# Leaving out GpSimd's spacer memset behind the row gathers of thirteen of sixteen sequences

## The reference, cut to what matters

```python
# third layer: two of eight experts for each token, weighted, plus the shared experts p
y_sel = y_all[topk_idx, jnp.arange(T)[:, None], :]
y = (y_sel * topk_w[..., None]).sum(1).reshape(b, s, h)
y = y + p
...
# fourth layer: the gates come from the mean over a whole sequence of y
pooled = x.mean(axis=1)
logits = pooled @ gate_w.T + gate_b
...
gates = jax.nn.softmax(masked, axis=-1)
expert_out = jax.nn.gelu(jnp.einsum('bsd,eod->beso', x, expert_w) + expert_b[None, :, None, :], approximate=False)
return jnp.einsum('be,beso->bso', gates, expert_out)
```

## Time and profile before

| | |
|---|---|
| median of 3 runs | 590.78 us (590.07 to 592.22) |
| profiled execution, first to last instruction (span) | 585.8 us |
| what lies around the span | 590.78 - 585.8 = 5.0 us |
| POOL busy over the span | 232.9 us (40%), 319 instructions |
| PE busy over the span | 558.2 us (95%) |
| the 64 gathers of the last stage | starts from 468.9 to 566.6 us |

### The profile page before, as it was taken

One profiled execution on the slowest core, in us unless ns is written; L12 is line 12 of the kernel. 1 busy time (PEld: TensorE's weight loads), 2 busy tenths in 40 slices (PEclk: granted clock), 3 DMA queues, 4 the chain that ended last, 5 costly groups with the idle time before them and its releaser, 6 DMA issues.

```text
span 585.8 us, 11495 instructions
## 1 busy us (share of the span) xinstructions
PE 558.2 (95%) x3816; PEld 462.9 (79%) x3816; DVE 319.7 (55%) x967; ACT 242.6 (41%) x670; POOL 232.9 (40%) x319
## 2 busy tenths in 40 slices
PE   7999999988999999999999999999999999999895
PEld 4788887744999999988788978888888887776674
DVE  3877757676332225743537754444444444666564
ACT  1555444660211111115544245555555455443342
POOL 2312211042111121007545375555555078777860
PEclk9999999999999999999999999999999999999999
DMA  5960000185995522513396035555555324555562
GB/s 144 390 289 4 1 1 2 63 368 243 333 328 199 184 85 73 155 64 74 72 296 210 0 82 158 157 159 161 161 161 148 99 81 126 170 173 184 158 190 75
DMA packets 51158, 88.16 MB, mean 150 GB/s; under 512 B 9202, under 2 KB 41843, under 8 KB 49556
## 3 DMA queue, kind: packets, MB, share of 16 engines
q1 hardware_dynamic: 42980, 65.16, 31.6%
q0 software_dynamic: 8112, 22.16, 15.7%
HBM read 62.25 MB, written 25.04 MB: 149 GB/s over the span
## 4 chain that ended last, share of the span: by engine, by line
PE 74%; POOL 8%; DVE 7%; issue 4%; DMA 4%; ACT 2%; SPq 1%; POOLq 0%; ACTq 0%; DVEq 0%
PE psum L1326 10%; PE psum L1339 9%; PE psum L1498 9%; PE psum L1586 9%; POOL arena L924 6%; PE psum L1600 5%; PE psum L1182 5%; PE psum L1154 5%; PE psum L1515 4%; PE psum L1578 3%; DMA arena<-x,row_tok 2%; PE psum L1162 2%; PE psum L1661 1%; PE psum L1533 1%; POOL iota_i L954 1%
## 5 line engine op out<-in xcount | busy, mean ns | idle before, releaser
L924 POOL DMA_INDIRECT arena<-x,row_tok x71 | 68.3, 963 | 53.4 <-PE psum L1578 43.4
L924 POOL DMA_INDIRECT arena<-y_sorted,pos_k_i x64 | 64.4, 1006 | 34.7 <-issue 16.2
L1586 PE MATMUL psum<-big_w,arena 128*128 x284 | 73.0, 379 | 0.0
L1916 ACT ACTIVATE arena<-psum,arena 128x128 f32<-128x128 f32 x64 | 18.3, 368 | 106.4 <-PE psum L1326 84.7
L1661 PE MATMUL psum<-big_w,arena 128*128 x248 | 61.3, 379 | 0.0
L1326 PEld LDWEIGHTS psum<-arena,big_w 128*128 128x128 f32 x512 | 59.5, 192 | 1.7 <-issue 1.0
L1326 PE MATMUL psum<-arena,big_w 128*128 128x128 f32 x512 | 59.8, 275 | 0.8 <-DVE arena L2613 0.8
L1498 PE MATMUL psum<-arena,big_w 128*128 128x256 f32 x256 | 59.8, 381 | 0.2 <-ACT arena L1935 0.2
L1586 PEld LDWEIGHTS psum<-big_w,arena 128*128 128x128 f32 x284 | 53.7, 190 | 7.3
L1339 PE MATMUL psum<-arena 128*128 128x256 f32 (+1 forms) x256 | 57.7, 379 | 0.0
L2849 DVE SCALAR_TENSOR_TENSOR arena<-arena 128x128 f32<-128x128 f32 x71 | 20.8, 293 | 60.4 <-ACT arena L2002 57.2
(11 more groups left out here) (338 smaller groups left out, 996.3 us busy)
## 6 DMA issues: line engine op xcount, KB each, us to landing
y_sorted<-arena SPq DMA_DIRECT2D x71, 128.0 KB
big_w<-w SPq DMA_DIRECT2D x8, 1024.0 KB, 5.2
tokens<-x SPq DMA_DIRECT2D x4, 1024.0 KB, 13.2
x<-tokens SPq DMA_DIRECT2D x16, 256.0 KB, 2.6
z_kept<-arena SPq DMA_DIRECT2D x16, 256.0 KB
out<-arena SPq DMA_DIRECT2D x15, 256.0 KB
y_late<-arena SPq DMA_DIRECT2D x16, 128.0 KB, 1.7
big_w<-expert_w_t SPq DMA_DIRECT2D x1, 2048.0 KB, 8.0
```

The source lines that it names most:

```text
L924: pool.indirect_dma_start(dst, None, rows, bass.IndirectOffsetOnAxis(ap=idx, axis=0)).then_inc(done, 16)
L1586: mm = pe.matmul(bank[2 + i % RT][:, 0:2 * M1], c_gt[i % RT][:, k, :], mgu_s[:, k, bass.ds(e, 1), :].rearrange("p a m -> p (a m)"), start= ...
```

## The change

The call of space() in the last stage gets a condition. The memset, and POOL's wait for it, stay behind the twelve gathers of sequences 0 to 2, and go behind the 52 gathers of sequences 3 to 15. Gathers, their waits for d_z, and all other engines' programs are as before.

```diff
                 for n, k, done in parts:
                     gather_rows(yk[b % RT][:, 2 * n + k, :], y2_dram, pos_k_i[:, b * NB + n, k:k + 1], done)
-                    space()
+                    if b < RT:
+                        space()
```

## The result

The first runs of the changed kernel took 603.74 us in the median (601.26 to 606.12, 4 runs), those of the kernel before beside them 590.42 us (589.92 to 592.22, 4 runs): a ratio of 1.0215, 95% interval 1.0179 to 1.0250. That is slower, and outside the range that was given. So this part has two things to explain: what the change does, and what the first runs had that the later ones had not.

A forecast was written before the change was run, and what follows sets the result against it. POOL's spaced gathers were taken to bound the last stage from sequence 10 on, costing 3.67 us over the loop's beat. Removing that whole cost: 590.78 - 3.67 = 587.1 us, 0.6% less; range 586.0 to 591.0 us.

The forecast's parts named there:

- The bound in the kernel before: Last stage: POOL's gathers need 6.43 us per sequence, the loop 5.35, so POOL sets the beat from sequence 10 on.
- the lead: How far a sequence's last gather starts ahead of its sum: 10.42 us at sequence 3, 3.95 at sequence 9.
- The unspaced gap of 0.30 us: POOL's pause between gathers without a memset, taken from an earlier stage; the change saves 0.19 us per gather.
- 3.67 us: Last stage: what gathers cost over eleven steps, 62.52 us against 58.85; the most that faster gathers can give.
- The 5.0 us "around the span": Median of the runs above the profiled span of 585.8 us; claimed that nothing of it changes.
- What else feels it: Side effects: gather landing covered (4.84 us against a 7.2 us lead), DVE's sums not slowed by memsets, nothing gained in the loop.
- the beat of 5.35 us: Last stage: time per sequence of the loop without POOL, transposes to sum, expected to hold up to sequence 14.
- the eleven steps: PE's transposes from sequence 3 to 14, last stage: 62.52 us before, 58.85 at the loop's beat.
- the last sentence of the signs: Prediction wrong too if the loop's beat moves from 5.35 us; each 0.1 us is 1.1 us in eleven steps.
- Rival 2: Unspaced gathers and DVE hinder each other; if every gather took 1.42 us, 598.0 us; chance 0.10.
- Rival 1: The gap between POOL's gathers takes the memset's place; time near 590.8 us, or 588 to 590 if part won; chance 0.15.
- rival 3: Gathered rows land late, beyond 7.2 us, as closer gathers queue in the DMA engines; 588 to 591 us; chance 0.04.

The follow-up runs named there:

- g2: The kernel before, unchanged, run for its profile on the third set's chip: 587.64 us, one run.
- g1: The changed kernel again, unaltered, on a third chip: 581.60 us, 0.9901 of the kernel before.
- g3: The kernel before with two spacers behind each gather of sequences 3 to 15: 601.08 us, 1.0233 of the kernel before.
- h1: The changed kernel once more, unaltered, to meet the slow occasion again: 582.80 us, 0.9926 of the kernel before.
- m1: The changed kernel without added copies, in the sixth set: 581.59 us, 0.9919 of the kernel before.
- f1: The changed kernel word for word, in the second set: 581.57 us, 0.9925 of the kernel before.
- m2: The changed kernel plus 512 KB of DRAM copies per sequence, on the sixth set's chip: 582.46 us, 0.9917 of the kernel before.
- k2: The kernel before plus 512 KB of DRAM copies per sequence, in the fifth set: 588.46 us, 1.0011 of the kernel before.
- e2: The changed kernel, but POOL waits for the sum of sequence b - 2 in place of b - 3: 581.89 us, 0.9911 of the kernel before.
- m3: The changed kernel with POOL's wait for the sum of b - 2, plus 512 KB of copies per sequence: 583.35 us, 0.9941 of the kernel before.
- k1: The changed kernel plus 512 KB of DRAM copies per sequence, in the fifth set: 597.15 us, 1.0189 of the kernel before.

## Why the prediction was right or wrong

**Right, and shown.** The bound in the kernel before (POOL's interval of 1.565 us uses up the lead, then sets the beat): g2 shows the same idle times of DVE, g1 has none on the same chip, and g3, with an interval of 1.874 us, pays for it. The unspaced gap of 0.30 us: in every trace of the change, 1.25 us a gather where nothing lengthens it; the mean interval of gathers 12 to 63 in g1 is 1.367 us (1.375 forecast). That the lead stays long and costs nothing: it settles at 9.5 us (10.5 forecast). That nothing but this changes on the four chips of the later runs: PE's transposes in g1 are 5.35 us apart up to sequence 14.

**Right in the time, not in the sign.** The first gather of a sequence was to name DVE's sum as its releaser. In g1, h1 and m1 one gather does, in f1 none: POOL's own lengthened gathers hold it 0.7 us behind the limit.

**Mis-sized.** The term "3.67 us" was that of one execution. In g2 it is 4.62 us, and the medians differ by 4.3 (h1) to 5.8 us (m1): 0.9901 to 0.9926 where 0.9938 was forecast. The prediction named this as the reason of its lower end. The 5.0 us "around the span" are misread as well: in every run that has both figures, launch time less span is 1.7 to 1.9 us. The profiled execution, with its span of 585.8, was by that one of about 587.6 us, some 3 us quicker than the median run, and the other 3 us of the 5.0 lie inside the spans of the slower executions. So the loss was read from an execution that was not the median one.

**Wrong.** The range, 586.0 to 591.0, missed the first result by 12.7 us, and the step that failed is "What else feels it", with the beat of 5.35 us that it leaves untouched. It looked for contention in two places, the landing of rows (against the lead) and the length of DVE's operations, and put the rest of the loop, PE and ACT, at no change without a reason. The first result has 72.94 us for the eleven steps in place of 58.85. It is waits for PE that end late there, by 1.3 to 3.5 us, in four places of the stage (at 498, 520 to 526, 541 to 547 and 560 to 566 us), and since the loop is one serial chain from transposes to sum, they lengthen it, with the lower clock behind them. None of the rivals was this; only the last sentence of the signs, that the beat itself might move, covers it, with no mechanism and no chance of its own. Rival 2, the slower one, had the sign and another mechanism: gathers of 1.42 us in most places, while in the first result no more gathers are lengthened than in g1 and POOL waits for DVE. That both came out slower is chance. Rival 1 and rival 3 do not show either: no sum waited for a gather.

**What stays open.** Why PE's signals are late on those two occasions. The runs exclude as causes that are enough by themselves: the unspaced gathers, their number in a row, the long lead, the first twelve spacers (each present in kernels at 0.99), and added memory traffic (m2). They do not exclude any of them as a part of the cause on a slow occasion. Something outside the program is needed, a chip or an occasion: 22 runs of the change on four chips lie between 580.35 and 583.90 us, its first 4 between 601.26 and 606.12. On such an occasion the kernel before is not hit in the same way. Beside the first result it took 590.42 us, 1.9 to 3.5 more than in the six sets, with two late signals outside the last stage; in k2, with the copies, it stands at 1.0011. So the change has a part in the loss after all, as has the occasion; which part could not be tried, because e2 and m3 never met such an occasion, nor the change without the copies the chip of k1. Whether a shorter lead guards against it is therefore open too. That the lost semaphore records and the late signals have one cause is only a guess from their coming together on both occasions; the two traces of the kernel before have the lost records too, one with two late signals and one (k2) with none. All runs here come with a granted clock and a span, so they do not tell either whether the recording itself takes part.

**Versions.** e2 (no spacer from sequence 3 on, the earlier wait) is at 0.9911 twice, the change at 0.9901 to 0.9926: no difference that these intervals show. On five chips every version with fewer or smaller spacers beats the kernel before by 0.6 to 1%; on the two slow occasions the kernel before was the better by 2%.

## What to carry to other kernels

A spacer on a queue costs what it adds to the interval between the real instructions, here 0.19 us of its 0.49, and only from the point on where the queue's lead is used up; the lead, row by row against its consumer, tells where that is. A serial loop over engines has no cover for a late signal: in this stage late signals, with the lower clock behind them, cost some 17 us; at 284 us of the kernel before, where PE had other work queued, they left no pause of PE. And a surprising result wants the same program run again on another chip before its cause is sought in the code: here four variants all seemed to cure a loss that the changed kernel itself did not show on its next four chips.

## What the runs showed of the hardware

On two occasions of seven, what waited for a TensorE matmul started 1.3 to 3.5 us later than usual in several places (ACT's copy 4.24 us after the start of the transposes, in place of 0.75): in the last stage only in the changed kernel, in an earlier stage of the first occasion in both kernels (ACT's copy 4.46 us after the start of its matmuls in the kernel before, in place of 2.03). The granted clock fell to a share of 0.80 to 0.97 in the stretches with these pauses; in g3, where PE idles 2.2 us in most steps, it fell too (0.986 to 0.994 over the whole run against 0.995 to 0.999 for the kernel before beside it). Two memsets in a row with a wait each take 0.48 us together and one takes 0.22; the gap in front of a gather is 0.27 us behind one as behind two, and 0.50 in some places of g3.
